# Two pieces of VectorE's work given to GpSimd, and three activation-table loads moved or merged, in a four-layer block

## The reference

```python
x = x + tanh(g0) * attention_mix(ln(x), ctx, Wq, bq, Wk, bk)   # softmax(q k^T) of ctx mixes the rows of ln(x)
x = x + tanh(f0) * ternary_ffn(ln(x), w_gate_up, w_proj)       # weights quantised to -1, 0, 1 by groups of 64
x = x + tanh(g1) * state_space(ctx, ln(x), ...)                # below; ln(x) is the gate z
x = x + tanh(f1) * mixture_of_experts(ln(x), ...)              # 64 experts, 8 for each token

def state_space(ctx, z):
    xin = in_proj_w @ ctx                                      # 256 channels
    u = silu(sum_k conv_w[:, k] * xin[:, l - 3 + k] + conv_b)  # causal convolution, 4 taps
    dt, B, C = split(x_proj_w @ u)
    delta = softplus(dt_proj_w @ dt + dt_proj_b)
    state = state * exp(delta * A) + delta * u * B             # 16 states for each channel, over 256 steps
    return (state @ C + D * u) * silu(z)
```

## Time and profile before

| | us |
|---|---|
| time, median of 3 runs | 412.1 |
| time, lowest and highest | 411.82, 413.02 |
| span of the profiled execution, first to last instruction | 411.6 |
| VectorE busy | 305.4 |
| ScalarE busy | 263.1 |
| GpSimd busy | 260.1 |
| TensorE busy | 338.7 |

### The profile page before, as it was taken

One profiled execution on the slowest core, in us unless ns is written; L12 is line 12 of the kernel. 1 busy time (PEld: TensorE's weight loads), 2 busy tenths in 40 slices (PEclk: granted clock), 3 DMA queues, 4 the chain that ended last, 5 costly groups with the idle time before them and its releaser, 6 DMA issues.

```text
span 411.6 us, 7573 instructions
## 1 busy us (share of the span) xinstructions
PE 338.7 (82%) x2217; PEld 267.8 (65%) x2217; DVE 305.4 (74%) x694; ACT 263.1 (64%) x530; POOL 260.1 (63%) x213
## 2 busy tenths in 40 slices
PE   4945974698789799989885189999999999999980
PEld 2431663256566567666685178899998899899870
DVE  2999999979999999999888946554544535454365
ACT  0899999999888898888264344445445544554410
POOL 4200022679996897788423588778788787878730
PEclk9995895599999989989999579999999999999997
DMA  8930530577344877441198339899898989865557
GB/s 235 372 121 0 152 114 3 183 224 244 118 153 130 273 259 260 154 146 59 42 263 204 104 105 209 219 212 241 202 238 219 221 216 217 224 139 94 96 107 241
DMA packets 59132, 72.17 MB, mean 175 GB/s; under 512 B 6802, under 2 KB 43458, under 8 KB 59106
## 3 DMA queue, kind: packets, MB, share of 16 engines
q1 hardware_dynamic: 49104, 56.04, 44.2%
q0 software_dynamic: 8832, 15.74, 19.1%
q10 hardware_dynamic: 1170, 0.08, 0.3%
HBM read 61.75 MB, written 10.09 MB: 175 GB/s over the span
## 4 chain that ended last, share of the span: by engine, by line
PE 50%; ACT 15%; DVE 14%; DMA 12%; issue 5%; POOL 2%; SPq 1%; DVEq 0%; POOLq 0%; ACTq 0%
PE bank L1328 13%; PE bank L1366 10%; PE bank L1321 6%; PE bank L1162 5%; DMA ssm<-bc_rows 4%; PE bank L1308 3%; DVE bank L1565 3%; DMA B_last<-bc_rows 3%; ACT ssm L862 2%; ACT L862 2%; DVE ssm L1570 2%; ACT L900 2%; DMA du<-sums 2%; PE bank L1104 2%; PE bank L1314 1%
## 5 line engine op out<-in xcount | busy, mean ns | idle before, releaser
L602 POOL TENSOR_TENSOR ssm<-ssm,arena 128x1024 f32<-128x1024 f32 x31 | 73.2, 2360 | 18.8 <-DVE ssm L1570 9.3
L1570 DVE TENSOR_TENSOR_SCAN ssm<-ssm,bank 128x512 f32<-128x512 f32 x64 | 78.1, 1220 | 4.6 <-issue 2.3
L675 POOL DMA_INDIRECT ssm<-routed,idx x64 | 65.0, 1016 | 21.8 <-issue 14.6
L1793 DVE SCALAR_TENSOR_TENSOR ssm<-ssm,bank 128x96 f32<-128x96 f32 x64 | 20.1, 314 | 75.3 <-ACT ssm L974 75.0
L686 POOL DMA_INDIRECT sums<-ssm,idx x40 | 65.3, 1631 | 13.6 <-issue 10.4
L1328 PE MATMUL bank<-ssm,wguT 128*128 128x256 bf16 x576 | 72.4, 272 | 0.3 <-DVE ssm L1785 0.3
L1328 PEld LDWEIGHTS bank<-ssm,wguT 128*128 128x128 bf16 x576 | 56.0, 97 | 12.3 <-DVE ssm L1785 0.7
L974 ACT ACTIVATE ssm<-bank 128x96 f32<-128x96 f32 x64 | 16.1, 251 | 74.3 <-PE bank L1366 74.3
L1162 PE MATMUL bank<-xs,wguT 128*128 128x512 bf16 x192 | 49.4, 412 | 7.8 <-POOL xs L589 4.2
L1366 PE MATMUL bank<-arena,ssm 128*128 (+1 forms) x256 | 53.3, 331 | 1.8 <-ACT ssm L957 1.1
L862 ACT ACTIVATE ssm<-delta,A_sb 128x510 f32<-128x510 f32 x64 | 43.9, 714 | 6.1 <-DVE ssm L1570 5.9
(11 more groups left out here) (226 smaller groups left out, 667.9 us busy)
## 6 DMA issues: line engine op xcount, KB each, us to landing
ssm<-bc_rows SPq DMA_DIRECT2D x22, 512.0 KB, 3.8
arena<-bc_rows SPq DMA_DIRECT2D x16, 512.0 KB, 5.1
arena<-in_L_ffn_gate_proj SPq DMA_DIRECT2D x32, 192.0 KB
arena<-in_L_ffn_up_proj SPq DMA_DIRECT2D x32, 192.0 KB
arena<-in_L_ffn_down_proj SPq DMA_DIRECT2D x32, 192.0 KB
B_last<-bc_rows SPq DMA_DIRECT2D x10, 512.0 KB, 3.8
sums<-zero_f SPq DMA_DIRECT2D x1, 2304.0 KB, 14.0
arena<-in_L_ffn_w_gate_up SPq DMA_DIRECT2D x1, 2048.0 KB, 11.6
```

The lines of the kernel that those rows point to most:

```text
L602: pool.tensor_tensor(prod[:, a:b, :], hs[:, a:b, :], C_all[:, 2 * (q % 8):2 * (q % 8) + 2, :], ALU.mult).then_inc(s.prod_ok, 1)
L675: pool.indirect_dma_start(out=xe[:, k, :], out_offset=None, in_=routed, in_offset=bass.IndirectOffsetOnAxis(ap=idx2[:, k, 0:1], axis=0)).t ...
L1570: dve.tensor_tensor_scan(hs[:, k % 4, :], dA[:, k % 3, :], x[:, :], 0.0, ALU.mult, ALU.add).then_inc(s.scan_ok, 1)
```

## The change

Five edits.

1. VectorE no longer makes the first norm's eight rows; GpSimd does, with the same instruction (`normalise`), four behind each of the two deviations, which are now computed one at a time.
2. VectorE convolves only the first half of the channels (`convolve_first`). GpSimd convolves the second (`convolve_second`) behind the rows. It multiplies each tap into `delta[:, 1]`, which is free then, and adds it to the sum in a second instruction, where VectorE did both in one.
3. ScalarE's Silu of the second half waits for the last of GpSimd's seven instructions.
4. ScalarE asks for its first table set at the head of its program, ahead of the wait for the padding.
5. Ahead of softplus' Exp it asks for a set that has both Exp and Ln.

```diff
@@ gpsimd
-            ln_rstd(1)
+            def normalise(c):
+
+                pool.wait_ge(s.ln_r, c + 1)
+                for j in range(4 * c, 4 * c + 4):
+                    pool.tensor_scalar(xn[j], x_res[:, j, :], mv[:, j, 0:1], rstd[:, j:j + 1], ALU.subtract, ALU.mult).then_inc(s.xn_sb, 1)
+
+            def convolve_second():
+
+                pool.wait_ge(s.ld_cols, 16 * 4)
+                pool.wait_ge(s.wT_sb, 3)
+                pool.wait_ge(s.xin_sb, 4)
+                ub, tap = (v[:, 1, :].rearrange("p (b l) -> p b l", l=L) for v in (u, delta))
+                for k in range(DC):
+                    src = xin[:, 1, :, k:k + L]
+                    if k == 0:
+                        pool.tensor_scalar(ub, src, conv_sb[:, 1, 0:1], cols[:, 1:2], ALU.mult, ALU.add).then_inc(s.conv_second, 1)
+                    else:
+                        if k > 1:
+                            pool.wait_ge(s.conv_second, 2 * k - 1)
+                        pool.tensor_scalar(tap, src, conv_sb[:, 1, k:k + 1], None, ALU.mult).then_inc(s.conv_second, 1)
+                        pool.wait_ge(s.conv_second, 2 * k)
+                        pool.tensor_tensor(ub, tap, ub, ALU.add).then_inc(s.conv_second, 1)
+
+            ln_rstd(1, (0,))
+            normalise(0)
+            ln_rstd(1, (1,))
+            normalise(1)
+            convolve_second()
@@ scalar
+            act.preload_act_table_set("exp_and_others")
             act.wait_ge(s.c_pad, 1)
...
             for h in halves:
-                act.wait_ge(s.conv, 4 * h + 4)
+                act.wait_ge((s.conv, s.conv_second)[h], (DC, 2 * DC - 1)[h])
                 act.activation(u[:, h, :], u[:, h, :], ACT.Silu).then_inc(s.u_sb, 1)
...
+            act.preload_act_table_set("natural_log_exp_and_others")
             for h in halves:
                 act.wait_ge(s.sp_abs, 2 * h + 2)
                 act.activation(delta[:, h, :], delta[:, h, :], ACT.Exp, scale=-1.0).then_inc(s.sp_exp, 1)
@@ vector
             statistics(1)
-            normalise(1, 0)
-            normalise(1, 1)
             dve.wait_ge(s.ld_cols, 16 * 4)
             dve.wait_ge(s.wT_sb, 3)
-            def convolve(h):
+            def convolve_first():
...
-            convolve(0)
+            convolve_first()
             scales(0)
...
-            convolve(1)
             scales(1)
```

More of the change, by code:

```diff
@@ L146, in __init__ @@
         self.conv = sem("conv")
+        self.conv_second = sem("conv_second")
         self.xn1T_ps = sem("xn1T_ps")
@@ L1410, in _ @@
         def _(dve):
[L1411 to L1415, removed]
             def statistics(n, update=None, updated=None, chunks=(0, 1)):
@@ L1444, in _ @@
             statistics(1)
-            normalise(1, 0)
-            normalise(1, 1)
             dve.wait_ge(s.ld_cols, 16 * 4)
             dve.wait_ge(s.wT_sb, 3)
-            def convolve(h):
-                dve.wait_ge(s.xin_sb, 2 * h + 2)
-                ub = u[:, h, :].rearrange("p (b l) -> p b l", l=L)
+            def convolve_first():
+                dve.wait_ge(s.xin_sb, 2)
+                ub = u[:, 0, :].rearrange("p (b l) -> p b l", l=L)
                 for k in range(DC):
-                    src = xin[:, h, :, k:k + L]
+                    src = xin[:, 0, :, k:k + L]
                     if k == 0:
-                        dve.tensor_scalar(ub, src, conv_sb[:, h, 0:1], cols[:, h:h + 1], ALU.mult, ALU.add).then_inc(s.conv, 1)
+                        dve.tensor_scalar(ub, src, conv_sb[:, 0, 0:1], cols[:, 0:1], ALU.mult, ALU.add).then_inc(s.conv, 1)
                     else:
-                        dve.wait_ge(s.conv, 4 * h + k)
-                        dve.scalar_tensor_tensor(out=ub, in0=src, scalar=conv_sb[:, h, k:k + 1], in1=ub, op0=ALU.mult, op1=ALU.add).then_inc(s.conv, 1)
+                        dve.wait_ge(s.conv, k)
+                        dve.scalar_tensor_tensor(out=ub, in0=src, scalar=conv_sb[:, 0, k:k + 1], in1=ub, op0=ALU.mult, op1=ALU.add).then_inc(s.conv, 1)
             def scales(part2):
```

## The result

The changed kernel takes 421.21 us (median of 4 runs, 420.58 to 422.0) beside 412.42 for the kernel before, run next to it: ratio 1.0185, 95% interval 1.0144 to 1.0225. It is slower by 1.9%, and 6 us above the top of the forecast range. The profiled span went from 411.6 to 419.6 us.

A forecast was written before the change was run, and what follows sets the result against it. ScalarE, then TensorE, was taken to bound the first 90 us, VectorE the state loop after. Saving 1.28 us by a table load and losing 0.9 to collisions gave -0.4: 411.7 us for 412.1, range 410.7 to 415.0.

The forecast's parts named there:

- What GpSimd takes on: Price of GpSimd's one-input instructions in norm and convolution: 0.45 us for 256 elements, 1.2 us for 1,024.
- rival 1: GpSimd too slow, its convolution half late for ScalarE's Silu: 413.7 us, at the upper bound 420; chance 0.20.
- The collisions: GpSimd and VectorE block each other at their shared port, delaying ScalarE's spread of the first scales by 0.9 us.
- The alternation: A GpSimd row slips in ahead of each of VectorE's three long convolution instructions: 1.35 us.
- The small scaling: VectorE's instruction that finishes the scales is held by GpSimd's first sum: 0.6 us later, taken as 0.4.
- slack S1: VectorE's first scales are ready 0.75 us before ScalarE takes them up, at 25.11 for 25.86.
- rival 2: Collisions of GpSimd and VectorE cost less than slack S1: -1.28 to -0.9 us, 410.8 to 411.2; chance 0.20.
- Rival 3: GpSimd keeps the port pair, its rows served before VectorE's convolution: net -0.4 to +1.8 us; chance 0.11.
- The load: ScalarE's table load at 70.35, ahead of the decays, goes: sixth scan 1.28 us earlier, 1.04 of idling stays.
- rival 4: Shorter idling brings TensorE's upper clock sooner in the first gate product: at most 1.04 us more, 410.7; chance 0.06.
- The sum: Whole kernel: -1.28 + 0.9 = -0.4 us on a 411.6 span; the median lies 0.5 above it, so 411.7.
- The moves that were priced at nothing: Work taken from VectorE before 45.82, as the convolution's second half, and the early first table: worth 0.

The follow-up runs named there:

- f_all: The changed kernel with GpSimd's rows as (x + (-mean)) * rstd and its taps as (x * w) + 0.0; ratio 0.9985 to the kernel before.
- f_rows: The changed kernel with only GpSimd's rows rewritten, as (x + (-mean)) * rstd, taps left as they were; ratio 1.0107 to the kernel before.

## Why the prediction was wrong

**The step that failed** is the price under "What GpSimd takes on". The missing form was bounded by a cast from below and a two-input product from above, and the one-input instruction was put near the cast "because there is one stream to read". Measured: 2.84 us for 1.2 for a scaled tap, 1.3 for 0.45 for a row, both above the upper bounds (2.36 and 0.77). That a one-input instruction cannot cost more than a two-input one was the hidden assumption; in these rows of GpSimd the operations decide (a multiply alone took 2.85 us, a two-input addition 2.34), not the number of streams. The one scaling with multiply and add was right, 1.19 for 1.2. f_all, in which only the form is changed, removes the loss.

**What followed was rival 1** in kind: the half is late and ScalarE waits for it, 7.50 us. It was given 0.20, because its condition hung on the price above. That its "some 8 us, 420" at a scaling of 2.36 is so near the measured 8.0 us of span and 421.2 is in part luck, for it is put together in another way. It had four slow scalings and the last sum held back by two masks. Measured, the half is done at 44.97 for 34.5: 3.4 us because the rows ahead of it are slow (it begins at 25.53 for 22.1), 4.9 by three slow taps (the first scaling was fast), and 2.1 because the last tap, not the last sum, was held by the first mask.

**A second path was overlooked.** "The energies start at about 22.6 for 22.17 ... VectorE wants them only at 26: nothing" was true for rows of 0.45 us, but ScalarE needs them too: its spread also waits for the first of the energies (`act.wait_ge(s.en_ps, 1)`), and its copies of the transposed rows stand ahead. With rows of 1.3 us that cost 1.82 us, and 0.00 in f_rows. The prediction asked what late taps would cost, but not what late rows would.

**The collisions.** The alternation was right, its price too high at one place. Three GpSimd rows were to put 1.35 us on VectorE's three instructions; f_all shows 0.54 (4.46 for 3.92), f_rows 0.18 (4.10) and the changed kernel 0.10. It is GpSimd that pays (four rows in 5.46 us for 2.16). The small scaling's 0.64 was as its working had it (0.6; the sum took 0.4 for it). Together the spread was 0.45 late, not 0.9. The rows alone stayed inside the slack S1, as rival 2 had it (0.00 in f_rows); with the small scaling's wait it was used up. Rival 3 did not come.

**The tables.** The load was saved as forecast, and rival 4 came on top: 1.94 us from the loop's first product to the sixth scan are saved, for 1.28. The idle ahead of the scan is 0.40, not 1.04. Rival 4 was given 0.06, though the earlier trace rows showed a product behind 4.21 us of idling, and the earlier trace rows a low clock over it. That the shorter idling is what raised the clock stays likely, not shown.

**The sum with measured terms.** With the fast form: -1.94 + 0.51 = -1.4 us, -0.35%; f_all measured -0.15% (-0.42 to +0.11). With the form as written: +9.61 - 1.83 + 0.36 of the later copy = +8.1; the span rose by 8.0. The 0.5 us by which the prediction's sum goes from the span to the median came from different executions: in each run here the time is 1.7 to 1.9 above the span of the same execution. As the sum works by differences, nothing of the forecast hangs on it. The moves that were priced at nothing gave nothing: no kernel reaches the first spread or the loop sooner by work taken from VectorE.

## What to carry to other kernels

Before work is moved to another engine, find or measure exactly this form there, with the same operations, not only the same shape; the number of inputs gives no bound. Work that is taken from an engine that is not waited for earns nothing, and gives the new engine two ways to cost: its own speed where a late result is wanted, and the long two-input instructions of both, which hold each other up. When a price is unsure, work out for everything that waits for the result what happens if the price is several times too low; here two such waits, for the rows and for the half, made up the loss.

## What the runs showed of the hardware

- GpSimd's `tensor_scalar` over 128x1024 f32: 1.19 us for multiply with add or add with multiply, 2.85 for a multiply alone, 3.79 with a subtract in the pair; over 256 elements 0.55, 0.93, 1.23. A two-input addition over 1,024 took 2.34. An added 0.0 makes a multiply 2.6 times as fast (1.11 us).
- Side by side with VectorE's two-input instructions, short GpSimd ones go from 0.64 to 1.30 us each and cost VectorE little (8.61 us for six, 1.43 for 1.31 each); long ones stretched three of VectorE's from 3.92 to 6.63 and 7.39.
- VectorE's small scaling (0.20 us) was held to the end of a GpSimd sum that was running: 0.82, 0.84, 1.54 and 1.99 us. Beside a tap with a multiply alone (f_rows) it took 0.20; why it was free there was not followed.
- The first gate product behind 2.78 us of idling ran at a granted clock of 0.54 to 0.67 (4.98 to 4.03 us, five kernels), behind 4.21 us at 0.50 to 0.53 (5.28 to 5.09 us, three kernels).
